# Two weight-remainder splits of a gated cross-attention block, moved from VectorE to GpSimd

## The chip, the cores and the metric

The kernel runs on one core of a Trainium2 chip, written directly against the engines: each engine has its own instruction list, executes it in order, and waits on semaphores. The metric is device time in microseconds (us) of one execution; lower is better. "DVE" is VectorE, "PE" TensorE, "ACT" ScalarE, "POOL" GpSimd, "SP" SyncE (it only issues DMAs here).

## The reference

One Flamingo-like layer: layer norm, fp8-quantised projections, self attention and cross attention with grouped heads, an fp8 output projection behind a tanh gate, and then a mixture of eight experts, two for each token. The change touches the first half only:

```python
x = x + tanh(g_xattn) * xattn(layernorm(x), ctx)   # 8 batches of 112 tokens, 375 context rows, width 512
    ln_out = ln(hidden)
    q, qx = fp8_linear(ln_out, wq), fp8_linear(ln_out, wqx)   # 16 heads of 128 each
    k, v  = fp8_linear(ln_out, wk), fp8_linear(ln_out, wv)    # 8 groups of 128 each
    kx, vx = split(ctx @ w_kv_x.T)                            # 8 groups of 128 each
    q, k, qx, kx = ln over each head's 128 channels
    cat = concat(gqa(q, k, v), gqa(qx, kx, vx))
    out = fp8(cat / smooth) @ wproj * scale
x = x + tanh(g_ffn) * experts(layernorm(x))
```

## The kernel before, in words

The attention stage walks over four group pairs (`gp` = 0 to 3) and, within each, over eight batches: 32 steps. A step projects batch `s` (`project`, six products `j` = 0 to 5: q, qx, k with v, and three chunks of the context) and attends for the batch before it, `t` = `s` - 1. Every engine has its own `step` function with a hand-written order; `passes` calls them in the same sequence on each engine.

Products are taken in fp32 by two halves. A weight block `w_raw` (in the tile `shared`) is copied by ACT into a rounded half `w_hi` (`w_high`, L600), and the remainder `w_lo` = `w_raw` - `w_hi` is a subtraction (`split_low`, L492, called from `w_low`). The weights of a group pair come in four parts, by the product that uses them (`USED`): part 0 (q) and part 1 (qx), each of 4 x 512 = 2048 elements in each of the 128 partitions; part 2, the two pieces k and v, two instructions of 4 x 256 = 1024 elements; part 3 (kx and vx, the context), one instruction of 2048. `project(s, n)` of the first step of a new group pair waits for `wh_done[n]` and `wl_done[n]`.

At a change of group pair two steps are special. The last step of the old group pair has `change == "old"`, the first step of the next has `change == "new"`. There are three such boundaries. In the kernel before DVE makes all four remainders there: part 0 in the middle of the "old" step, part 1 ahead of `sums(s, 5)`, part 2 behind `scale(s, 5)`, and part 3 in the "new" step, behind `sums(s, 1)`. Only in the very first step of the stage does POOL make part 2.

What DVE does around these places: `sums` (L859) adds up the squares of a projected head, `scale` (L868) multiplies by the reciprocal deviation, `rounded` (L918, L920, L923, L925, L928) rounds the attention output of batch `t` to fp8, `max_self` (L874) and `max_cross` (L888) take maxima of scores, `norm_self` (L880, L882) and `norm_cross` (L893, L895) scale the softmax.

What POOL does in each step: `c_low(s, k)` for k = 0, 1, 2 (L566, the remainder of a context chunk of 500 elements in each partition), each followed by `rstd(s, j)`, which is an addition `va` (L556, it waits for `sums(s, j)`) and a power `rs` (L560); then `rstd` 3, 4 and 5. `scale(s, j)` on DVE waits for `rs`, and PE's transposes of the heads (`turn`) wait for `scale`: `turn(t, 3)`, between `project(s, 1)` and `project(s, 2)`, waits for `scale(t, 5)`.

PE's order in a step: `project(s,0)`, `turn(t,0)`, `turn(t,1)`, `project(s,1)`, `turn(t,2)`, `turn(t,3)`, `project(s,2)`, `score_self(t)`, `score_cross(t,0)`, `score_cross(t,1)`, `turn(t,4)`, `project(s,3)`, `turn_self(t)` and so on (L718 are the matmuls of products 0 to 2, L727 those of 3 to 5, L747 and L751 `turn`, L759 and L766 the scores).

SP fetches the weights of the next group pair (`load_w`) behind the waits for all `wh_done` and `wl_done` of the current one, and behind the context loads and the output stores of the first two batches.

Of the kernel before, what the change touches and what calls it, by code (L numbers as in the profile page):

```python
# [369 lines left out]
def flat(ap):  # L370
    return ap.rearrange("p a b -> p (a b)")
# [17 lines left out]
def attention(nc, c, sb, ps, sem, ctxT, wproj, catd, vec, ident, mhalf, epst, xq, smi,  # L389
# [73 lines left out]
    def passes(eng, step):  # L463

        step(0, 0, None, 0, "first", None)

        def batches(gp):
            s0 = gp * B  # L470
            with eng.Fori(0, 2) as i:
                s = s0 + 2 * i
                step(s + 1, 1, s, gp + 1, None, None)
                step(s + 2, 0, s + 1, gp + 1, None, i)
            step(s0 + 5, 1, s0 + 4, gp + 1, None, 2)
            step(s0 + 6, 0, s0 + 5, gp + 1, None, 3)
            step(s0 + 7, 1, s0 + 6, gp + 1, "old", None)

        with eng.Fori(0, GP - 1) as gp:
            batches(gp)  # L480
            step(gp * B + B, 0, gp * B + 7, gp + 1, "new", None)
        s0 = (GP - 1) * B
        with eng.Fori(0, 3) as i:
            s = s0 + 2 * i
            step(s + 1, 1, s, None, None, None)
            step(s + 2, 0, s + 1, None, None, None)
        step(s0 + 7, 1, s0 + 6, None, None, None)
        step(None, 0, s0 + 7, None, None, None)

    def split_low(eng, n):  # L490
        for lo, hi in USED[n]:
            last = eng.tensor_tensor(w_lo[:, :, lo:hi], w_raw[:, :, lo:hi], w_hi[:, :, lo:hi].bitcast(F32),  # L492
                                     ALU.subtract)
        return last

    @block.sync
    def _(sp):
        def load_w(gp):
            for n in range(len(USED)):
                sp.wait_ge(wl_done[n], gp)  # L500
                sp.wait_ge(wh_done[n], gp)
            for k in range(KB):
                weights.fetch(sp, gp, k)

        def load_c(s, b, k):

            sp.wait_ge(ch_done, 3 * s + k + 1)
            sp.wait_ge(cl_done, 3 * s + k + 1)
            sp.dma_start(c_raw[:, k, :, :], ctxT[b, k]).then_inc(c_in_done[k], 16)

        def store(st):
            sp.wait_ge(ct_done, st + 1)
            sp.dma_start(catd[st], cat[:, :]).then_inc(cat_out, 16)

        sp.sem_inc(cat_out, 16)


        for gp in range(GP):
            s0 = gp * B
            for b in range(2):  # L520
                for k in range(NC):
                    load_c(s0 + b, b, k)
                if gp > 0:
                    store(s0 + b - 2)
            if gp + 1 < GP:
                load_w(gp + 1)
            else:


                for n in range(len(USED)):  # L530
                    sp.wait_ge(wl_done[n], GP)
                    sp.wait_ge(wh_done[n], GP)
                for n in range(4):
                    sp.dma_start(shared[:, n * D:(n + 1) * D], wproj[0, n]).then_inc(wp_load[n], 16)
                sp.wait_ge(cat_out, 16 * (B + 1))
                sp.dma_start(cat_tile(shared), catd[0:B].rearrange("b p n -> p b n")
                             ).then_inc(cat_load[0], 16)
            with sp.Fori(2, B) as b:
                for k in range(NC):
                    load_c(s0 + b, b, k)  # L540
                store(s0 + b - 2)
        store(GP * B - 2)
        store(GP * B - 1)
        sp.wait_ge(cat_out, 16 * (GP * B + 1))

    @block.gpsimd
    def _(pool):
        pool.sem_inc(cl_done, 3)
        pool.sem_inc(va_done, 6)
        pool.sem_inc(rs_done, 6)  # L550

        def rstd(s, j):

            rows, lo, hi = STAT[j]
            pool.wait_ge(rd_done, 6 * (s + 1) + j + 1)
            pool.tensor_tensor(va[0:rows, lo:hi], ss[0:rows, lo:hi], epst[0:rows, lo:hi],  # L556
                               ALU.add).then_inc(va_done, 1)
            pool.wait_ge(va_done, 6 * (s + 1) + j + 1)
            pool.wait_ge(ln_done, 6 * s + j + 1)
            pool.tensor_tensor(rs[0:rows, lo:hi], va[0:rows, lo:hi], mhalf[0:rows, lo:hi],  # L560
                               ALU.pow).then_inc(rs_done, 1)

        def c_low(s, k):
            pool.wait_ge(ch_done, 3 * (s + 1) + k + 1)
            pool.wait_ge(pj_rdy, 6 * s + 4 + k)
            pool.tensor_tensor(flat(c_lo[:, k, :, :]), flat(c_raw[:, k, :, :]),  # L566
                               flat(c_hi[:, k, :, :]).bitcast(F32), ALU.subtract).then_inc(cl_done, 1)

        def w_low(g, n):

            pool.wait_ge(wh_done[n], g + 1)
            split_low(pool, n).then_inc(wl_done[n], 1)

        def step(s, par, t, g, change, k):
            if change == "first":
                w_low(g, 2)
            if s is None:
                return
            for j in range(3):
                c_low(s, j)  # L580
                rstd(s, j)
            for j in range(3, 6):
                rstd(s, j)

        passes(pool, step)

    @block.scalar
# [240 lines left out]
    def _(v):  # L828
# [10 lines left out]
        def smooth_of(g):  # L839
            v.wait_ge(ya_done, 2 * B * g + 2)  # L840
            v.tensor_copy(smg[:, :], smi[:, bass.ds(g, 1), :].rearrange("p a b -> p (a b)"))

        def w_low(g, n):

            v.wait_ge(wh_done[n], g + 1)
            split_low(v, n).then_inc(wl_done[n], 1)
# [8 lines left out]
        def sums(s, j):  # L855
            rows, lo, hi = STAT[j]
            v.wait_ge(pj_done, 6 * (s + 1) + j + 1)
            v.wait_ge(va_done, 6 * s + j + 1)
            v.tensor_reduce(ss[0:rows, lo:hi],  # L859
                            sq[0:rows, j % 2, 0:(hi - lo) * HD].rearrange("p (h d) -> p h d", d=HD),  # L860
                            AX, ALU.add).then_inc(rd_done, 1)
# [9 lines left out]
        def max_self(t):  # L871
            v.wait_ge(ss_rdy, t + 2)
            v.wait_ge(es_done, t + 1)
            v.tensor_reduce(nmax[0:T, 0:HP], p_self[0:T, 0:HP * T].rearrange("p (h d) -> p h d", d=T),  # L874
                            AX, ALU.max, negate=True).then_inc(ms_done, 1)
# [54 lines left out]
        def step(s, b_next, t, g, change, k):  # L930

            A, Q = s is not None and change != "first", t is not None
            if A: sums(s, 0)
            if A: sums(s, 1)
            if change == "new": w_low(g, 3)
            if Q: max_self(t)
            if A: scale(s, 0)
            if Q: max_cross(t, 0)
            if Q: max_cross(t, 1)
            if Q: norm_self(t)  # L940
            if Q: norm_cross(t, 0)
            if Q: norm_cross(t, 1)
            if Q: take_self(t)
            if A: sums(s, 2)
            if Q: take_cross(t, 0)
            if Q: max_cross(t, 2)
            if A: scale(s, 1)
            if Q: take_cross(t, 1)
            if Q: max_cross(t, 3)
            if A: scale(s, 2)  # L950
            if A and b_next is not None: inputs(s + 1, b_next)
            if Q: norm_cross(t, 2)
            if Q: norm_cross(t, 3)
            if k is not None: weights.means(v, g, k)
            if change == "old": w_low(g, 0)
            if A: sums(s, 3)
            if Q: smoothed(t, 0)
            if Q: take_cross(t, 2)
            if Q: take_cross(t, 3)
            if A: scale(s, 3)  # L960
            if A: sums(s, 4)
            if Q: smoothed(t, 1)
            if A: scale(s, 4)
            if change == "old": w_low(g, 1)
            if A: sums(s, 5)
            if A: scale(s, 5)
            if change == "old": w_low(g, 2)
            if Q: rounded(t)
            if change == "new": smooth_of(g)
            if change == "first":  # L970
                w_low(g, 0)
                w_low(g, 1)
                w_low(g, 3)
                smooth_of(g)
                for j in range(6):
                    sums(s, j)
                    if j > 0:
                        scale(s, j - 1)
                    if j == 3:
                        inputs(s + 1, b_next)  # L980
                scale(s, 5)
# [736 lines left out]
```

## Time and profile before

| | |
|---|---|
| median of 3 runs | 1292.58 us (1290.19 to 1293.03) |
| the profiled execution | 1290.19 us, its span 1288.5 us |
| mean granted TensorE clock over the span | 0.95 |
| attention stage, about 57 to 872 us of the span | PE busy 770.71 of 814.70 us, DVE 643.90, ACT 520.72, POOL 353.05 |

A profile row gives the start or the sum in us, the duration, the engine, the line of the kernel and the tiles written and read. What stands in brackets behind a row of the timeline is how long the engine sat idle before it and what ended that wait. A row's duration runs from the start of the instruction to its end; when an engine is held up after it has begun an instruction, the hold-up is inside that duration.

### The profile page before, as it was taken

The page shows a single profiled execution, that of the slowest core. Times are in us where ns is not written, and L with a number is a line of the kernel's source. Part 1 is how long each engine was busy: PE and PEld are TensorE (multiplying, and loading weights), DVE is VectorE, ACT ScalarE, POOL GpSimd, SP SyncE. Part 2 cuts the span into 40 slices and gives each one's busy share as a digit, 9 for nine tenths or more (in the row PEclk, how much of TensorE's full clock was granted, in tenths as well). Part 3 has the DMA queues.
Part 4 walks back from the last instruction along what each step waited for, and adds up shares of the span by engine and source line. Part 5 has one row for each costly group of instructions (what it writes and reads, how often), then busy time and mean ns, then how long its engine had stood idle before and what let it go on. Part 6 is the DMA issues. An engine that isn't in the chain of part 4 may idle for free. (4 is left out here: it accounts for less than half of the span.)

```text
span 1288.5 us, 22449 instructions
## 1 busy us (share of the span) xinstructions
PE 1128.0 (88%) x5792; PEld 912.7 (71%) x5792; DVE 862.1 (67%) x1742; ACT 698.1 (54%) x1747; POOL 478.4 (37%) x608
## 2 busy tenths in 40 slices
PE   1089999989999989999998999996999449999996
PEld 1078777767787767877776788884887337777885
DVE  7968778886888787878888887775444555646100
ACT  7955677844757765567674664652122303333342
POOL 3074344343443443434434444440000202656432
PEclk9589999999999999999999999998999659999999
DMA  4041111114111113211111411102464606766220
GB/s 189 24 164 47 31 42 45 40 33 164 52 42 31 47 33 146 67 31 55 40 32 32 137 47 31 54 16 71 151 201 148 212 25 188 212 176 179 56 41 1
DMA packets 51715, 107.36 MB, mean 83 GB/s; under 512 B 5984, under 2 KB 26464, under 8 KB 49568
## 3 DMA queue, kind: packets, MB, share of 16 engines
q1 hardware_dynamic: 46912, 97.00, 23.3%
q0 software_dynamic: 4704, 9.18, 3.1%
q8 instruction: 45, 0.74, 0.2%
q14 instruction: 54, 0.44, 0.1%
HBM read 91.48 MB, written 16.52 MB: 84 GB/s over the span
## 5 line engine op out<-in xcount | busy, mean ns | idle before, releaser
L718 PE MATMUL p_proj<-w_hi,xqs 128*112 128x256 f32 (+1 forms) x512 | 173.8, 358 | 56.9 <-DVE w_lo L492 47.6
L566 POOL TENSOR_TENSOR c_lo<-c_raw,c_hi 128x500 fp32r<-128x500 f32 x96 | 122.2, 1273 | 174.9 <-ACT c_hi L606 174.9
L727 PE MATMUL p_proj<-w_hi,c_hi 128*125 128x512 f32 x384 | 167.5, 436 | 9.2 <-DVE w_lo L492 8.2
L556 POOL TENSOR_TENSOR va<-ss,epst 112x4 f32<-112x4 f32 (+2 forms) x192 | 75.7, 394 | 262.3 <-DVE ss L859 262.2
L718 PE MATMUL p_proj<-w_lo,xqs 128*112 128x256 f32 (+1 forms) x512 | 164.0, 339 | 0.0
L560 POOL TENSOR_TENSOR rs<-va,mhalf 112x4 f32<-112x4 f32 (+2 forms) x192 | 153.5, 800 | 18.0 <-POOL va L556 5.8
L727 PE MATMUL p_proj<-w_lo,c_hi 128*125 128x512 f32 x384 | 153.5, 400 | 0.0
L727 PE MATMUL p_proj<-w_hi,c_lo 128*125 128x512 f32 x384 | 153.4, 399 | 0.0
L718 PEld LDWEIGHTS p_proj<-w_hi,xqs 128*112 128x112 f32 x512 | 90.2, 176 | 73.5 <-issue 55.5
L859 DVE TENSOR_REDUCE ss<-sq 112x4 f32<-112x512 f32 (+2 forms) x192 | 96.0, 503 | 54.6 <-ACT sq L627 53.7
L655 ACT ACTIVATE pcross<-p_cross,nmax 112x375 f32<-112x375 f32 x128 | 73.1, 573 | 80.9 <-DVE nmax L888 79.8
L718 PEld LDWEIGHTS p_proj<-w_lo,xqs 128*112 128x112 f32 x512 | 90.5, 177 | 11.7
L766 PE MATMUL p_cross<-kxT,qxT 128*112 128x375 f32 x256 | 98.0, 485 | 0.0
L1127 PE MATMUL p_acc<-p_hi,p_catr 128*128 128x512 f32 x224 | 88.5, 395 | 9.1 <-DVE p_lo L1166 9.1
L727 PEld LDWEIGHTS p_proj<-w_hi,c_hi 128*125 128x125 f32 x384 | 72.8, 189 | 28.9 <-issue 10.3
L627 ACT ACTIVATE sq<-p_proj 112x512 f32<-112x512 f32 (+2 forms) x192 | 90.3, 471 | 0.0
L1127 PE MATMUL p_acc<-p_lo,p_catr 128*128 128x512 f32 x224 | 88.1, 393 | 0.0
L156 ACT ACTIVATE shared<-shared,w_mean,wsc 128x128 f32<-128x128 f32 (+1 forms) x160 | 65.9, 486 | 39.6 <-DVE w_mean L140 39.6
L727 PEld LDWEIGHTS p_proj<-w_lo,c_hi 128*125 128x125 f32 x384 | 72.9, 190 | 18.0
L727 PEld LDWEIGHTS p_proj<-w_hi,c_lo 128*125 128x125 f32 x384 | 72.4, 188 | 18.2
L792 PE MATMUL p_out<-pcrossT,valx 125*128 125x224 f32 x384 | 83.1, 352 | 0.0
L911 DVE TENSOR_TENSOR yb<-p_out,smg 128x448 bf16<-128x448 f32 x64 | 39.7, 620 | 56.6 <-PE p_out L792 56.6
(232 smaller groups left out, 2711.3 us busy)
## 6 DMA issues: line engine op xcount, KB each, us to landing
c_raw<-in_ctxT SPq DMA_DIRECT2D x96, 250.0 KB, 2.6
shared<-in_w_in SPq DMA_DIRECT2D x16, 1024.0 KB, 9.1
shared<-in_wproj SPq DMA_DIRECT2D x32, 256.0 KB, 3.0
raw_g<-in_Wg SPq DMA_DIRECT2D x8, 1024.0 KB
raw_u<-in_Wu SPq DMA_DIRECT2D x8, 1024.0 KB, 7.6
raw_d<-in_Wd SPq DMA_DIRECT2D x8, 1024.0 KB, 5.7
cat_scratch<-cat SPq DMA_DIRECT2D x32, 224.0 KB, 2.0
shared<-cat_scratch SPq DMA_DIRECT2D x2, 1792.0 KB, 8.5
```

The lines of the kernel that those rows point to most:

```text
L156: act.activation(cols, cols, ACT.Identity, bias=mean, scale=self.wsc[:, n, block_k])
L556: pool.tensor_tensor(va[0:rows, lo:hi], ss[0:rows, lo:hi], epst[0:rows, lo:hi], ALU.add).then_inc(va_done, 1)
L560: pool.tensor_tensor(rs[0:rows, lo:hi], va[0:rows, lo:hi], mhalf[0:rows, lo:hi], ALU.pow).then_inc(rs_done, 1)
L566: pool.tensor_tensor(flat(c_lo[:, k, :, :]), flat(c_raw[:, k, :, :]), flat(c_hi[:, k, :, :]).bitcast(F32), ALU.subtract).then_inc(cl_done, 1)
L627: act.activation(sq[0:rows, j % 2, 0:n], bank[0:rows, 0:n], ACT.Square, scale=float(HD) ** -0.5).then_inc(pj_done, 1)
L655: act.activation(pcross[0:T, h, :], p_cross[0:T, h % 2, 0:TC], ACT.Exp, bias=nmax[0:T, 4 + h:5 + h], accum_out=lsum[0:T, 4 + h:5 + h]).the ...
L718: m = pe.matmul(bank[0:T, o:o + w], xqs[:, n, k, :], (w_hi, w_lo)[i % 2][:, k, lo:lo + w], start=(i == 0), stop=(i == 2 * KB - 1))
L727: m = pe.matmul(bank[0:CT, :], a[:, ch, k, :], w[:, k, CKX:CV], start=(i == 0), stop=(i == 3 * KB - 1))
L766: pe.matmul(p_cross[0:T, h % 2, 0:TC], qxT[:, h * T:(h + 1) * T], kxT[:, h // HPG, :], start=True, stop=True).then_inc(sx_rdy, 1)
L792: m = pe.matmul(p_out[:, HPG * T:2 * HPG * T], valx[0:CT, par, k, g * P:(g + 1) * P], flat(pcrossT[0:CT, k, HPG * g:HPG * (g + 1), :]), st ...
L859: v.tensor_reduce(ss[0:rows, lo:hi], sq[0:rows, j % 2, 0:(hi - lo) * HD].rearrange("p (h d) -> p h d", d=HD), AX, ALU.add).then_inc(rd_don ...
L1127: m = pe.matmul(acc[:, j, :], catr[:, n % 2, j * P:(j + 1) * P], w[:, n % 2, :], start=(first and part == 0), stop=(last and part == 1), s ...
```

## The change

POOL makes part 3 in the "new" step, behind `c_low(s, 1)` and `rstd(s, 1)`, and part 2 at the end of the "old" step, behind `rstd(s, 5)`. DVE's two calls go. Parts 0 and 1 stay on DVE where they were. The arithmetic, the semaphores and what waits on them stay.

```diff
@@ pool step
             for j in range(3):
                 c_low(s, j)
                 rstd(s, j)
+                if j == 1 and change == "new":
+                    w_low(g, 3)
             for j in range(3, 6):
                 rstd(s, j)
+            if change == "old":
+                w_low(g, 2)
@@ vector step
             if A: sums(s, 0)
             if A: sums(s, 1)
-            if change == "new": w_low(g, 3)
             if Q: max_self(t)
             if A: scale(s, 0)
...
             if change == "old": w_low(g, 1)
             if A: sums(s, 5)
             if A: scale(s, 5)
-            if change == "old": w_low(g, 2)
             if Q: rounded(t)
             if change == "new": smooth_of(g)
```

## Rows read from the trace of the kernel before

**Rows 1.** Busy time of each engine over the span (first part of the page).
```profile
PE 1128.0 (88%) x5792; PEld 912.7 (71%) x5792; DVE 862.1 (67%) x1742; ACT 698.1 (54%) x1747; POOL 478.4 (37%) x608
```

**Rows 2.** Waits of PE, 57 to 900 us: total us, times, longest.
```profile
PE p_proj L718 <- DVE w_lo L492: 47.6, 7, 40.9
PE p_proj L727 <- DVE w_lo L492: 8.2, 3, 2.7
...
PE p_out L789 <- DVE pcrossT L906: 6.8, 13, 0.9
```

**Rows 3.** Timeline of PE at the first boundary: start, duration, instruction, idle before.
```profile
266.43 0.34 PE L718 MATMUL p_proj<-w_hi,xqs 128*112 128x256 f32 x1 [1.52 <-DVE w_lo L492]
...
273.67 0.76 PE L727 MATMUL p_proj<-w_hi,c_hi 128*125 128x512 f32 x1 [2.74 <-DVE w_lo L492]
274.22 0.63 PE L727 MATMUL p_proj<-w_lo,c_hi 128*125 128x512 f32 x1
...
276.73 0.39 PE L727 MATMUL p_proj<-w_lo,c_hi 128*125 128x512 f32 x1
```

**Rows 4.** Busy time and granted clock in two stretches: PE, PEld, DVE, ACT, POOL, clock.
```profile
274.00:276.00 2.00, 2.00 (x6) 1.50 (x6) 1.51 (x1) 1.45 (x8) 2.00 (x3) 0.50 0.00 0
...
280.00:282.00 2.00, 2.00 (x10) 1.49 (x10) 2.00 (x4) 0.66 (x2) 1.89 (x3) 1.00 0.00 0
```

**Rows 5.** Timeline of DVE at the first boundary.
```profile
263.59 0.43 DVE L868 TENSOR_TENSOR nkx<-nkx,rs 125x256 f32<-125x256 f32 x1 [1.08 <-POOL rs L560]
263.93 2.35 DVE L492 TENSOR_TENSOR w_lo<-shared,w_hi 128x1024 fp32r<-128x1024 f32 x2
266.20 1.46 DVE L918 TENSOR_SCALAR yb<-yb 128x896 bf16<-128x896 bf16 x1
267.69 0.40 DVE L920 TENSOR_SCALAR ye<-yb 128x896 uint16<-128x896 uint16 x1
...
271.03 2.28 DVE L492 TENSOR_TENSOR w_lo<-shared,w_hi 128x2048 fp32r<-128x2048 f32 x1
...
274.49 1.74 DVE L868 TENSOR_TENSOR nq<-nq,rs 112x512 f32<-112x512 f32 x1 [0.64 <-POOL rs L560]
...
277.26 0.62 DVE L882 TENSOR_TENSOR pself<-pself,linv 112x448 f32<-112x448 f32 x1
```

**Rows 6.** Timeline of POOL at the first boundary.
```profile
262.86 0.70 POOL L560 TENSOR_TENSOR rs<-va,mhalf 125x2 f32<-125x2 f32 x1
265.95 1.45 POOL L566 TENSOR_TENSOR c_lo<-c_raw,c_hi 128x500 fp32r<-128x500 f32 x1 [2.40 <-ACT c_hi L606]
270.61 2.77 POOL L556 TENSOR_TENSOR va<-ss,epst 112x4 f32<-112x4 f32 x1 [3.20 <-DVE ss L859]
...
274.43 1.26 POOL L566 TENSOR_TENSOR c_lo<-c_raw,c_hi 128x500 fp32r<-128x500 f32 x1
275.64 0.65 POOL L556 TENSOR_TENSOR va<-ss,epst 112x4 f32<-112x4 f32 x1
276.37 1.01 POOL L560 TENSOR_TENSOR rs<-va,mhalf 112x4 f32<-112x4 f32 x1
```

**Rows 7.** Timeline of DVE in the stage's first step.
```profile
62.83 4.49 DVE L492 TENSOR_TENSOR w_lo<-shared,w_hi 128x2048 fp32r<-128x2048 f32 x2 [0.27 <-ACT w_hi L600]
68.32 3.41 DVE L492 TENSOR_TENSOR w_lo<-shared,w_hi 128x2048 fp32r<-128x2048 f32 x1 [1.00 <-ACT w_hi L600]
71.66 2.30 DVE L841 COPY smg<-smi 128x8 f32<-128x8 f32 x1
```

**Rows 8.** Timeline of POOL in the stage's first step.
```profile
66.57 7.36 POOL L492 TENSOR_TENSOR w_lo<-shared,w_hi 128x1024 fp32r<-128x1024 f32 x2 [46.51 <-ACT w_hi L600]
```

**Rows 9.** Groups of POOL by line: busy us, mean ns.
```profile
L566 POOL TENSOR_TENSOR c_lo<-c_raw,c_hi 128x500 fp32r<-128x500 f32 x96 | 122.2, 1273 | 174.9 <-ACT c_hi L606 174.9
...
L556 POOL TENSOR_TENSOR va<-ss,epst 125x2 f32<-125x2 f32 x96 | 20.4, 212 | 247.7 <-DVE ss L859 247.7
```

**Rows 10.** Timeline of SP, the fetch of the next weights.
```profile
297.16 2.06 SPq L129 DMA_DIRECT2D shared<-in_w_in  x4
```

## The prediction, on record before the changed kernel ran

> **What bounds the kernel now.** I read the engines' busy time first, then PE's waits in the attention stage, then the timelines of PE, DVE and POOL around one change of group pair, and last the only place where POOL already makes a weight remainder. PE is busy 88% of the span, DVE 67% and POOL 37% [rows 1]. So PE sets the pace, and the 4.6 us that leave DVE at each boundary are worth only what PE waits for them; POOL has idle time enough, but the question is when it is idle.
>
> PE's waits name the remainder [rows 2]. The 40.9 us are the start of the stage, where the change does nothing. The three waits of L727, 8.2 us together, are `project(s, 3)` at the three boundaries, waiting for part 3. At the first boundary [rows 3] PE waits 1.52 us for part 2 and 2.74 us for part 3. Behind the last wait the granted clock is 0.50, that is the lower of the two levels, 1.2 GHz, and it is back at 1.00 later [rows 4]; a matmul of that stretch takes 0.63 us until, at 276.73, one takes 0.39 again [rows 3]. In the timeline six of them stand 0.43 us apart where 0.23 is usual (up to nine at the other boundaries), so the clock adds 1.2 to 1.8 us. What could be won at each boundary is thus 1.52 + 2.74 + about 1.2 = 5.5 us, and 16 us over the three. The other two boundaries repeat the first (three waits of L727, 8.2 us in sum, 2.7 the longest [rows 2]), so I work out one and take it three times.
>
> **The change, part by part.** The removal from DVE: two instructions of 1024 elements, 2.35 us, and one of 2048, 2.28 us, a boundary [rows 5].
>
> The price on POOL. No row shows a POOL subtraction of 2048 elements. Two rows bound it. The 500-element one takes 1.27 us and a two-element addition 0.21 us [rows 9], so an element costs (1.27 - 0.21) / 498 = 2.1 ns and 2048 cost 4.6 us. The two of 1024 elements in the first step took 7.36 us together [rows 8], but with DVE's subtractions in between: DVE's first pair ended at 67.32 and its third ran until 71.73 us [rows 7]. Read as turns taken, POOL's first ran from 67.32 to 69.59 (2.27 us), DVE's from there to 71.73 (2.14 of its usual 2.28), and POOL's second from 71.73 to 73.93 (2.2 us); the tiny copy on DVE at 71.66, 2.30 us long, ended with it. So 1024 elements cost 2.2 to 2.3 and 2048 about 4.5 us. That is twice DVE's price. The upper bound is 7.4 us for 2048, if the recorded duration is all work; the lower 4.1 us, from the slope between 1.27 us at 500 and 2.2 us at 1024. I take 4.5, which both readings give.
>
> Turns taken. The same is seen at the boundary. POOL's `c_lo` at 265.95 stretches DVE's L918, which ends 0.26 us behind it and takes 1.46 us [rows 5, 6] where 0.39 is its usual time; DVE's `w_lo` at 271.03 holds POOL's four-element `va` from 270.61 to 273.38; `c_lo` at 274.43 holds DVE's L868 of 274.49 until 275.69 and beyond that it needs 0.54 us; then `va` waits for it. Whoever is held goes next.
>
> The Trainium skill ("SBUF — State Buffer", section on the two separate sides) says the same: the port pair of VectorE and GpSimd is an exclusive lock for a whole instruction, also against a VectorE instruction with two SBUF inputs. It speaks against this change, and its "GPSIMD Engine Reference" (elementwise comparison) gives 4497 ns for 2048 fp32 elements on GpSimd and 2293 ns on VectorE; by that the sum below would stay within 0.1 us a boundary. The trace agrees with the second figure (2.28 us) and shows no row for the first.
>
> Now the new order at the first boundary. Both waits of the moved calls on `wh_done` are long fulfilled, so only POOL's own order and the turns count.
> - Part 2 can't start before `rs` of `rstd(s, 5)` ends, at 263.56 [rows 6]. First piece, 2.27: to 265.83. It starts a moment before DVE's `scale(s, 5)` (263.59), as `c_lo` does at 274.43, and holds it; that takes 0.4: to 266.2. Second piece, 2.2: to 268.4. So `project(s, 2)` starts at about 268.6 where it was 266.43: 2.1 us later. `turn(t, 3)`, which waits for `scale(s, 5)`, goes from 264.4 to 266.4 and stays hidden.
> - DVE's L918 gets the turn: to 268.7. Queued behind part 2 on POOL is `c_low(s, 0)`, 1.25: to 269.95. L920 is held and ends at 270.2. From the end of L920 to the start of `va` took 270.61 - 268.09 = 2.52 us (rest of `rounded`, `sums(s, 0)`): 272.75.
> - `va` now finds no `w_lo` on DVE and takes 0.2: to 272.95. This is all that the relief of DVE brings POOL: 0.43 us against 273.38. From there to the end of `rs` of `rstd(s, 1)` it took 277.38 - 273.38 = 4.0: 276.95.
> - Part 3 can start there. DVE's L882, 1.03 us behind the end of L868, comes at nearly the same moment and takes 0 to 0.6 us of it: 277.4. Part 3, 4.5: to 281.9. PE follows 0.36 us behind the remainder, as now (271.03 + 2.28 to 273.67): 282.3.
>
> So `project(s, 3)` starts 8.6 us later than at 273.67. Of this, 2.2 us is the slower engine, and 6.4 us the later start, 277.4 instead of 271.03, because part 3 stands behind `rstd(s, 1)` and the whole chain before it behind part 2. PE has nothing to do between `turn(t, 4)` and then. The lower clock stays about as it is: the wait is longer, the number of matmuls until it rises again I take as the same, with 0 to 0.5 us more. Given back: after the wait DVE and ACT are ahead, and PE's small waits in the rest of the step go, 0 to 0.5 us. Behind part 3 on POOL stand `c_low(s, 2)`, needed by `project(s, 5)` 8 us later, and `rstd(s, 2)`, whose `sums` waits for PE anyway: nothing. On DVE the `norm_cross` instructions are held during part 3, but PE's `turn_self` follows `project(s, 3)`, 3.5 to 4 us long, in which they catch up: nothing; without that cover they would cost 1 us. SP's fetch stands at 297.16 [rows 10], far behind part 3's semaphore: it moves with the rest, and no DMA is added.
>
> Sum: 3 x 8.6 - 3 x 0.1 = 25.5 us, or 1290.19 + 25.5 = 1315.7 for the profiled execution. That one was the fastest of three, 2.4 us under the median of 1292.58, so the median of the changed kernel lies between 1315.7 and 1318.1; I take 1317.
>
> **The rivals.**
> - No turns: the two engines run side by side, and the hold-ups above are something else. Then part 2 ends at 263.56 + 4.5 = 268.1, `c_low(s, 0)` at 269.4, and with 1.3 for `rstd(s, 0)`, 1.3, 1.3 for `rstd(s, 1)` and 4.5, part 3 ends at 277.7: 4.4 us later than now, 13 in all, 1304. Against it stand four stretched rows at one boundary [rows 5, 6], each ending within 0.3 us of the other engine's instruction or 0.54 behind it.
> - POOL's large subtraction costs its recorded 3.7 us for 1024 elements. Then part 2 adds 2.9 and part 3 2.9 us more: 14.4 us a boundary, 43 in all, 1333. Against it: the copy of eight elements that took 2.30 us on DVE beside it [rows 7], which only makes sense if it was held.
> - Absorbed, no change: PE makes up the delay from later waits. The largest of its waits in the stage that isn't for a weight remainder is 6.8 us in 13 times, the longest 0.9 [rows 2], and 8.6 would be needed behind each boundary.
> - The other side, faster: the remainders are done on POOL before PE asks, and all of the 5.5 us at a boundary go, 1290.19 - 16.4 = 1274. It decides at part 3's end: sooner than 273.31 is a gain. With both POOL prices at nothing, `rounded` would begin at 264.0, `sums(s, 0)` end at about 267.9 and `rstd(s, 1)` at about 272.0, so the prices together could be at most 1.3 us; DVE itself needs 4.6. Only if POOL's rows say nothing of these instructions can it be.
>
> The Trainium skill's "Perfetto Trace Analysis" (on ScalarE and DVE operations) reminds that moving work between GpSimd and VectorE might not help as they share a read port; as a rule it would leave the time about the same, which is the absorbed case.
>
> **How the numbers follow.** Forecast 0.82; no turns 0.07; the dearer subtraction 0.05; absorbed 0.04; faster 0.02. The forecast's own spread: price of part 3 4.1 to 5.2 (-0.4 to +0.7), part 2 the same again, L882's turn -0.5, clock and catching up -0.5 to +0.5: 7.2 to 10.5 us a boundary, 1312 to 1322 with the 2.4 us between runs. No more than 2 in 10 are to be left out; the errors of such a hand-made schedule run both ways, so I go to 1305 (the case without turns just touches it) and 1328. About 0.2% (2.6 us) is what a measurement of this kernel can tell from no change. Slower 0.94, the same 0.04, faster 0.02.
>
> **What would show each step.** PE's wait for `w_lo` should be put down to POOL: about 1.7 us before L718 (or more, if `turn(t, 3)` runs earlier) and 8 to 9.5 us before L727, three times. POOL should show L492 six times with 1024 elements, 2.2 to 2.3 us, and three times with 2048, 4.5 us (5.0 with L882's turn inside); DVE's L868 of `scale(s, 5)` should take 2.6 us there instead of 0.43, and L895 some 4 to 5 us during part 3. `va` of `rstd(s, 0)` should fall from 2.77 to 0.2 us. The expert stage should have the same length. I would be wrong if part 3 ended before about 278 us on the old time axis, that is if POOL reached it sooner than `rstd(s, 1)` lets me think, or if the two engines' instructions overlapped.

## The result, and the profile after

The changed kernel takes 1314.07 us in the median (1311.06 to 1315.18, 4 runs), the kernel before 1292.01 us beside it (1290.19 to 1293.03). The ratio is 1.0162, with a 95% interval of 1.0147 to 1.0175: slower by 22 us. Over all 13 runs of the changed kernel on record the median is 1312.82 us. The profiled execution took 1314.62 us, its span 1312.9 us, 24.4 us more than before.

Busy time of each engine over the span, and busy time and clock (0.50, the lower level) at the start of `project(s, 3)`:

```profile
PE 1133.0 (86%) x5792; PEld 918.1 (70%) x5792; DVE 877.1 (67%) x1733; ACT 699.7 (53%) x1747; POOL 497.0 (38%) x617
```
```profile
280.00:282.00 2.00, 1.81 (x4) 1.48 (x5) 1.96 (x4) 0.00 (x0) 1.05 (x1) 0.50 0.00 0
```

DVE has 9 instructions less than in [rows 1] and is busy 15 us more. What left it took 13.9 us; the rows count hold-up as busy time, so a busier DVE here is a DVE that is held.

PE's waits in the attention stage of the changed kernel, 57 to 920 us (total us, times, longest):

```profile
PE p_proj L722 <- DVE w_lo L492: 43.3, 4, 41.1
PE p_proj L731 <- POOL w_lo L492: 18.8, 3, 7.0
...
PE p_tr L755 <- DVE nkx L872: 4.6, 3, 1.7
```

The lines moved by 4, so L731 is the L727 of [rows 2]. PE's three waits for part 3 were 8.2 us and are 18.8, and they are POOL's now. They understate it: PE is also slow before the wait. At the first boundary `project(s, 2)` ran at the lower clock and took 3.44 us where it took 1.96 before, which shortens the wait behind it and costs nothing more, as POOL sets its end.

PE at the first boundary:

```profile
264.97 0.54 PE L755 MATMUL p_tr<-ident,nkx 125*128 125x125 f32 x3 [1.71 <-ACT kT L643]
267.19 0.53 PE L722 MATMUL p_proj<-w_hi,xqs 128*112 128x256 f32 x1 [1.69 <-ACT sq L631]
...
272.68 0.48 PE L755 MATMUL p_tr<-ident,nkx 125*128 125x125 f32 x3
280.19 0.76 PE L731 MATMUL p_proj<-w_hi,c_hi 128*125 128x512 f32 x1 [7.03 <-POOL w_lo L492]
280.75 0.63 PE L731 MATMUL p_proj<-w_lo,c_hi 128*125 128x512 f32 x1
...
284.41 0.39 PE L731 MATMUL p_proj<-w_lo,c_hi 128*125 128x512 f32 x1
```

The second wait, 1.69 us, is credited to ACT's second square of the step. But `project(s, 2)` needs only the first, and what it waits for besides, POOL's L492 pair, ended at 267.05 (next fence), 0.14 us ahead of it: a wait for several semaphores can carry the wrong name. Compare with [rows 3]: PE waits three times here, and the last wait is 7.03 us.

POOL at the first boundary:

```profile
261.53 0.70 POOL L560 TENSOR_TENSOR rs<-va,mhalf 125x2 f32<-125x2 f32 x1
262.19 4.86 POOL L492 TENSOR_TENSOR w_lo<-shared,w_hi 128x1024 fp32r<-128x1024 f32 x2
267.01 1.40 POOL L566 TENSOR_TENSOR c_lo<-c_raw,c_hi 128x500 fp32r<-128x500 f32 x1
271.18 0.20 POOL L556 TENSOR_TENSOR va<-ss,epst 112x4 f32<-112x4 f32 x1 [2.77 <-DVE ss L863]
...
275.34 4.50 POOL L492 TENSOR_TENSOR w_lo<-shared,w_hi 128x2048 fp32r<-128x2048 f32 x1
279.80 1.25 POOL L566 TENSOR_TENSOR c_lo<-c_raw,c_hi 128x500 fp32r<-128x500 f32 x1
```

DVE at the first boundary:

```profile
262.25 2.58 DVE L872 TENSOR_TENSOR nkx<-nkx,rs 125x256 f32<-125x256 f32 x1 [1.08 <-POOL rs L560]
264.76 2.54 DVE L922 TENSOR_SCALAR yb<-yb 128x896 bf16<-128x896 bf16 x1
267.33 1.33 DVE L924 TENSOR_SCALAR ye<-yb 128x896 uint16<-128x896 uint16 x1
...
275.26 6.27 DVE L886 TENSOR_TENSOR pself<-pself,linv 112x448 f32<-112x448 f32 x1
...
281.63 0.42 DVE L899 TENSOR_SCALAR pcross<-pcross,linv 112x375 f32<-112x375 f32 x1
```

The axis has slid by 1.33 us against [rows 6], so times are best counted from the end of `rs` of `rstd(s, 5)`: 263.56 before, 262.23 now. `project(s, 3)` started 10.11 us behind it and starts 17.96 us behind it, 7.85 us later; at the second boundary it is 7.84. Three times 7.85 is 23.6 of the 24.4 us. The rest is small terms: this execution was 1.33 us ahead when it came to the first boundary, and lost 2.0 us between the third `project(s, 3)` and the end of the stage.

### The profile page after: what moved, and what is told of

It reads as the page before. It is cut to its first block and busy times, and to the rows that moved or that the text cites. A ratio compares the mean times of both kernels' runs of the same rounds, so it can differ in the third digit from the quotient of the medians.

```text
span 1312.9 us, 22452 instructions
## 1 busy us (share of the span) xinstructions
PE 1133.0 (86%) x5792; PEld 918.1 (70%) x5792; DVE 877.1 (67%) x1733; ACT 699.7 (53%) x1747; POOL 497.0 (38%) x617
## 5 line engine op out<-in xcount | busy, mean ns | idle before, releaser
L722 PE MATMUL p_proj<-w_hi,xqs 128*112 128x256 f32 (+1 forms) x512 | 177.6, 364 | 57.4 <-DVE w_lo L492 43.3
L731 PE MATMUL p_proj<-w_hi,c_hi 128*125 128x512 f32 x384 | 167.6, 437 | 19.9 <-POOL w_lo L492 18.8
L556 POOL TENSOR_TENSOR va<-ss,epst 112x4 f32<-112x4 f32 (+2 forms) x192 | 65.4, 341 | 281.6 <-DVE ss L863 281.6
L722 PE MATMUL p_proj<-w_lo,xqs 128*112 128x256 f32 (+1 forms) x512 | 167.5, 345 | 0.0
L731 PE MATMUL p_proj<-w_hi,c_lo 128*125 128x512 f32 x384 | 153.5, 400 | 0.0
L731 PE MATMUL p_proj<-w_lo,c_hi 128*125 128x512 f32 x384 | 153.2, 399 | 0.0
L722 PEld LDWEIGHTS p_proj<-w_hi,xqs 128*112 128x112 f32 x512 | 93.0, 182 | 74.1 <-issue 55.9
L722 PEld LDWEIGHTS p_proj<-w_lo,xqs 128*112 128x112 f32 x512 | 93.2, 182 | 11.8
L731 PEld LDWEIGHTS p_proj<-w_hi,c_hi 128*125 128x125 f32 x384 | 72.7, 189 | 39.3 <-issue 21.0
L731 PEld LDWEIGHTS p_proj<-w_lo,c_hi 128*125 128x125 f32 x384 | 72.8, 189 | 18.0
L731 PEld LDWEIGHTS p_proj<-w_hi,c_lo 128*125 128x125 f32 x384 | 72.4, 189 | 18.3
```

The costliest lines, as they stand in the source:

```text
L722: m = pe.matmul(bank[0:T, o:o + w], xqs[:, n, k, :], (w_hi, w_lo)[i % 2][:, k, lo:lo + w], start=(i == 0), stop=(i == 2 * KB - 1))
L731: m = pe.matmul(bank[0:CT, :], a[:, ch, k, :], w[:, k, CKX:CV], start=(i == 0), stop=(i == 3 * KB - 1))
```

## The experiments

All were compared with the kernel before on the same chip. "Behind" means behind the end of `rs` of `rstd(s, 5)` at the first boundary.

**Part 2 alone on POOL.**

```diff
-                if j == 1 and change == "new":
-                    w_low(g, 3)
@@ vector step
             if A: sums(s, 1)
+            if change == "new": w_low(g, 3)
```

> Only part 2 goes to POOL; part 3 stays on DVE behind sums(s, 1). My theory (turns taken, and a chain through DVE's rounded): part 2 ends about 2.1 us later, the held rounded instructions bring sums(s, 1) to an end about 0.6 us later at most, DVE's 2.35 us are gained back only in part, and project(s, 3) starts 1.9 us later than before at each boundary: 5.8 us in all, about 1298. Rival, only the price of the engine counts (2.2 us for part 2, nothing for DVE's held instructions): DVE would reach part 3 2.3 us earlier and project(s, 3) would start 1 to 2 us earlier than before, 1287 to 1290.

Measured: 1298.11 us, ratio 1.0048 (1.0028 to 1.0067). PE in its trace:

```profile
267.72 0.53 PE L720 MATMUL p_proj<-w_hi,xqs 128*112 128x256 f32 x1 [1.69 <-ACT sq L629]
...
274.77 0.47 PE L729 MATMUL p_proj<-w_hi,c_hi 128*125 128x512 f32 x1 [1.10 <-DVE w_lo L492]
```

`project(s, 3)` starts 12.02 us behind, 1.9 later than before. DVE was relieved of 2.35 us and is nevertheless late for part 3: its rounding was held.

**Part 3 alone on POOL.**

```diff
-            if change == "old":
-                w_low(g, 2)
@@ vector step
             if A: scale(s, 5)
+            if change == "old": w_low(g, 2)
```

> Only part 3 goes to POOL, to the place it has in the change; part 2 stays on DVE. My theory: va of rstd(s, 0) starts at 270.61 as before but is no longer held, and from there the 9.0 us of the changed kernel lead to project(s, 3): at 279.6 instead of 273.67, 5.9 us a boundary, 17.8 in all, about 1310. Rival, the two moved parts cost alike because each is simply twice as dear on POOL (2.2 us each): about 6.6 us in all, 1299.

Measured: 1309.72 us, ratio 1.0137 (1.0118 to 1.0156).

```profile
279.51 0.76 PE L729 MATMUL p_proj<-w_hi,c_hi 128*125 128x512 f32 x1 [8.68 <-POOL w_lo L492]
```

16.04 us behind, 5.9 later than before. In the traces the two halves of the change add up: 1.9 + 5.9 = 7.8. (Between the medians they give 7.0 and 18.6 us, 3.6 more than the whole change.) Part 3 is three quarters of the loss, though both are the same number of elements.

**The later place without the slower engine.** Part 3 stays on DVE, behind `scale(s, 0)`.

```diff
             if A: sums(s, 1)
-            if change == "new": w_low(g, 3)
             if Q: max_self(t)
             if A: scale(s, 0)
+            if change == "new": w_low(g, 3)
```

> Nothing on POOL: part 3 stays on DVE but stands behind scale(s, 0), which waits for rs of rstd(s, 0). It is the later place without the slower engine. My theory: scale(s, 0) ends at about 273.7, part 3 at 276.0, project(s, 3) starts at 276.4, 2.7 us later than before, 8 us in all, about 1300. If the place were nothing and the engine all, it would stay at 1292.

Measured: 1301.09 us, ratio 1.0071 (1.0052 to 1.0089).

```profile
274.90 0.76 PE L727 MATMUL p_proj<-w_hi,c_hi 128*125 128x512 f32 x1 [5.26 <-DVE w_lo L492]
```

12.63 us behind, 2.5 later, and it costs more than that: `turn_self` starts 3.5 us later at this boundary, since all twelve matmuls of `project(s, 3)` ran at the lower clock. The median is 10.0 us above the kernel before, against 18.6 for part 3 on POOL: about half of what part 3 loses comes with a later place in the list alone. (The place in the change is later still, behind `rstd(s, 1)`.)

**The change, with `rounded` of the old step's batch moved.**

```diff
-            if Q: rounded(t)
+            if Q and change != "old": rounded(t)
...
             if Q: norm_cross(t, 3)
+            if change == "new": rounded(t - 1)
```

(`rounded` counts on a semaphore of its own for it.)

> The change as it is, but the rounding of the old group pair's last-but-one batch (rounded, 2.6 us alone, 5.8 us held) moves from the end of DVE's old step behind norm_cross(t, 3) of the new step. My theory: in the changed kernel POOL idles 2.77 us ahead of va of rstd(s, 0) because sums(s, 0) stands behind rounded; that idle goes, part 3 starts and ends about 3 us earlier, and 7 to 10 us of the 22 come back: 1304 to 1307. Rival, POOL's own work is the whole chain (price of its instructions): no change against 1314.

Measured: 1310.87 us, ratio 1.0131 (1.0102 to 1.0161), a miss: 3 us back instead of 7 to 10, and its interval overlaps that of the change.

```profile
279.89 0.76 PE L732 MATMUL p_proj<-w_hi,c_hi 128*125 128x512 f32 x1 [5.64 <-POOL w_lo L493]
...
301.06 0.46 PE L723 MATMUL p_proj<-w_hi,xqs 128*112 128x512 f32 x1 [3.44 <-issue]
```

The expected part did happen: POOL's idle ahead of `va` is gone and `project(s, 3)` starts 15.1 us behind (its `rs` ended at 264.80), 2.9 earlier than in the change. But at the head of the next loop pass PE idles 3.44 us where it was 1.08, and then runs at the lower clock. Busy time, clock and DMA share and GB/s of the 2 us before:

```profile
296.00:298.00 2.00, 1.62 (x8) 1.26 (x8) 0.72 (x3) 0.26 (x1) 0.89 (x2) 1.00 0.98 332
```

SP's list has the store of that batch ahead of three context loads. The store now waits until 294 us, and the loads fall on the loop's end.

**The same, with the stores behind both batches' loads.**

```diff
                     load_c(s0 + b, b, k)
-                if gp > 0:
-                    store(s0 + b - 2)
+            if gp > 0:
+                store(s0 - 2)
+                store(s0 - 1)
```

> The change with rounded moved (the kernel of 1310.87) and, in SP's list, the output stores of the last two batches placed behind the context loads of both first batches. In the former the store waits for the moved rounding until 294 us and the loads of batch 1 (1 MB in all) land at 294 to 298, when PE fetches the code of its next loop pass: its idle there is 3.44 us instead of 1.08, with the lower clock behind it. If that collision ate the gain, its two occurrences of 2.4 us and 1.3 us of clock come back: 1303 to 1305. Rival, the late rounding itself delays PE: no change, 1311.

Measured: 1305.03 us, ratio 1.0095 (1.0078 to 1.0112), as expected in size, with a less clean cause than that:

```profile
297.54 0.46 PE L724 MATMUL p_proj<-w_hi,xqs 128*112 128x512 f32 x1 [2.83 <-issue]
```

The idle at the head is 2.83, not 1.08; only 0.6 to 0.85 us of it at each of the two heads was the loads. The fall of the clock behind it is gone at the second head only: at the first the granted clock is 0.50 again from 299 to 301 us. And PE's waits for part 3 are 12.9 us in place of 14.8.

**Part 3 on DVE ahead of `rounded`, nothing on POOL.**

```diff
             if change == "old": w_low(g, 2)
+            if change == "old": w_low(g, 3)
             if Q: rounded(t)
...
-            if change == "new": w_low(g, 3)
```

> The kernel before with one call moved on DVE: part 3 directly behind part 2, ahead of rounded. PE's wait for part 3 (2.74 us and the lower clock behind it) goes. My theory: DVE's list is the second bound of the boundary, since PE's turn_self at 277.94 starts 0.06 us behind DVE's L882; that instruction stays where it is, so PE waits there instead and the time stays within 1 us a boundary of before, 1289 to 1293. Rival, PE's wait for the remainder is all that counts: 3.9 us a boundary, 11.8 in all, 1280.

Measured: 1291.66 us, ratio 0.9995 (0.9985 to 1.0005).

```profile
276.16 0.59 PE L773 MATMUL p_tr<-ident,pself 112*112 112x112 f32 x4 [3.83 <-DVE pself L882]
```

PE's wait for part 3 is gone from the list and comes back as 3.83 us ahead of `turn_self`, which starts 13.99 us behind, 0.4 earlier than before. DVE's list was the second bound: in the kernel before, L882 ended at 277.88 [rows 5], and `turn_self` began at 277.94.

**Part 3 at the head of POOL's new step**, part 2 on DVE.

```diff
@@ pool step
+            if change == "new":
+                w_low(g, 3)
             for j in range(3):
                 c_low(s, j)
```

> Part 2 stays on DVE; part 3 goes to POOL but to the head of its new step, ahead of c_low(s, 0), where POOL idles. If the later place were all of the loss, project(s, 3) would start at about 271 us and the kernel gain 3 us a boundary, 1283. My theory of turns taken: POOL gets its turn between DVE's two part 2 pieces at 265.1 and holds the second until 269.6, rounded, sums and the maxima come late, and PE waits for turn_self until about 281: 3 us a boundary later than before, 1301, still less than the 1310 of part 3 alone behind rstd(s, 1).

Measured: 1295.27 us, ratio 1.0022 (1.0013 to 1.0032). The rival's 1283 is out, and so is my 1301. POOL, DVE and PE, in this order:

```profile
264.09 5.03 POOL L492 TENSOR_TENSOR w_lo<-shared,w_hi 128x2048 fp32r<-128x2048 f32 x1 [0.94 <-ACT w_hi L602]
```
```profile
263.53 6.68 DVE L492 TENSOR_TENSOR w_lo<-shared,w_hi 128x1024 fp32r<-128x1024 f32 x2
```
```profile
270.35 0.53 PE L720 MATMUL p_proj<-w_hi,xqs 128*112 128x256 f32 x1 [5.84 <-DVE w_lo L492]
```

The turns came as thought (DVE's pair takes 6.68 us instead of 2.35), but `turn_self` was only 2.0 us late. That is what DVE's list gives: 4.33 us of hold-up on its pair, less the 2.28 us of part 3 that it no longer makes; I had left the second out. The other place of part 3 on POOL had ratio 1.0137: the place matters more than the choice of POOL.

**The turns alone.** Everything stays on DVE, and POOL makes part 2 once more behind `rstd(s, 5)`, into a tile that nobody reads.

```diff
+            if change == "old":
+                pool.wait_ge(wh_done[2], g + 1)
+                for n, (lo, hi) in enumerate(USED[2]):
+                    pool.wait_ge(sp_self, 2 * g - 2 + n)
+                    pool.tensor_tensor(spare[:, :, :], w_raw[:, :, lo:hi], w_hi[:, :, lo:hi].bitcast(F32),
+                                       ALU.subtract).then_inc(sp_self, 1)
```

> The kernel before, with all four parts on DVE, and POOL making part 2 once more, into a tile that nobody reads, at the place it has in the change (behind rstd(s, 5)). Only the turns between the two engines can cost anything. My theory: POOL's two pieces hold scale(s, 5) and then DVE's own part 2, which ends 4 to 5 us later, and PE's project(s, 2) and all behind it with it: 12 to 15 us in all, 1304 to 1307. Rival, the engines run side by side: nothing, 1292, or 1 us where c_low(s, 0) starts later.

Measured: 1303.30 us, ratio 1.0090 (1.0074 to 1.0107), just under what I expected. POOL, DVE and PE:

```profile
263.74 4.94 POOL L593 TENSOR_TENSOR spare<-shared,w_hi 128x1024 fp32r<-128x1024 f32 x2
```
```profile
263.81 2.64 DVE L879 TENSOR_TENSOR nkx<-nkx,rs 125x256 f32<-125x256 f32 x1 [1.09 <-POOL rs L565]
266.38 5.56 DVE L494 TENSOR_TENSOR w_lo<-shared,w_hi 128x1024 fp32r<-128x1024 f32 x2
```
```profile
272.09 0.52 PE L729 MATMUL p_proj<-w_hi,xqs 128*112 128x256 f32 x1 [4.97 <-DVE w_lo L494]
```

Work on an idle engine, for nobody, costs 11.4 us. That settles the rival without turns.

**A new order on DVE, nothing on POOL.** Part 1 goes ahead of `smoothed(t, 1)`, part 2 ahead of `scale(s, 5)`, part 3 to the head of the new step, `rounded` and SP's stores as above.

```diff
+            if change == "new": w_low(g, 3)
             if A: sums(s, 0)
...
+            if change == "old": w_low(g, 1)
             if Q: smoothed(t, 1)
             if A: scale(s, 4)
-            if change == "old": w_low(g, 1)
             if A: sums(s, 5)
-            if A: scale(s, 5)
             if change == "old": w_low(g, 2)
+            if A: scale(s, 5)
```

> The kernel before, nothing on POOL, DVE's list reordered at the boundary: part 1 ahead of smoothed(t, 1) where DVE idles 1.28 us, part 2 between sums(s, 5) and scale(s, 5) where it idles 1.08, part 3 at the head of the new step, rounded of the old step's batch behind norm_cross(t, 3), and the stores placed as in the run before. My theory: all three waits of PE (0.72, 1.52, 2.74) and the lower clock go, 4.4 + 1.2 us a boundary, less about 1 us for turn_self and the late rounding: 4.6 us, 14 in all, 1276 to 1281. Rival, DVE is bound through the boundary whatever its order, and PE waits elsewhere: 1290.

Measured: 1281.75 us, ratio 0.9916 (0.9899 to 0.9932); faster than both, just outside what I expected.

```profile
263.49 0.54 PE L753 MATMUL p_tr<-ident,nkx 125*128 125x125 f32 x3 [1.30 <-DVE nkx L870]
...
283.24 0.64 PE L791 MATMUL p_out<-pselfT,val 112*128 112x224 f32 x2 [0.86 <-DVE pcrossT L908]
...
287.38 0.46 PE L720 MATMUL p_proj<-w_hi,xqs 128*112 128x512 f32 x1 [2.37 <-issue]
```

No wait for a remainder is left at the boundaries. The loss is again at the loop's end.

**The same order, `rounded` and the stores in place.** Only the calls of the parts and of `scale(s, 5)` are moved, as in the diff above:

```diff
+            if change == "new": w_low(g, 3)
             if A: sums(s, 0)
...
+            if change == "old": w_low(g, 1)
             if Q: smoothed(t, 1)
...
             if change == "old": w_low(g, 2)
+            if A: scale(s, 5)
             if Q: rounded(t)
```

> The same new order of parts 1, 2 and 3 on DVE, but rounded at its old place at the end of the old step and SP as before. My theory: PE's waits for the parts go and come back as a wait for DVE's L882 ahead of turn_self, less the 1.3 to 2 us of idle that the new order fills on DVE: 1 to 2 us a boundary gained, 1286 to 1289. Rival, the order alone is worth all of the gain: 1282.

Measured: 1285.15 us, ratio 0.9952 (0.9935 to 0.9968), a little better than expected. PE still waits 1.16 us for part 3 at the first boundary, and then 2.00 us for L882 ahead of `turn_self` (3.83 with part 3 moved alone).

**The new order, `rounded` in two.** The stores stay behind both batches' loads. The clamp goes into a tile `yc` behind `norm_cross(t, 3)`, the other four instructions ahead of `smoothed(t, 1)`.

```diff
-            if change == "new": rounded(t - 1)
+            if change == "new": clamped(t - 1)
...
+            if change == "new": rounded_rest(t - 1)
             if Q: smoothed(t, 1)
```

> The reordered kernel of 1281.75, in which rounded of the old step's batch stands behind norm_cross(t, 3) and PE waits 0.9 us for take_cross(t, 3) and then 2.4 us at the head of the loop, where it waited 1.2. Here only the clamp (0.4 us, into a tile of its own) stays there, and the other four instructions stand ahead of smoothed(t, 1), where DVE idles. My theory: PE's wait before the loop's end is what lays its head's idle bare, so both go at the two loop heads and the first at the third boundary: 2 us a boundary and the lower clock at the heads, 5 to 8 in all, 1274 to 1277. Rival, the idle at the head comes from the stores that land just before it: 1 us a boundary, 1279.

Measured: 1274.76 us, ratio 0.9865 (0.9849 to 0.9882), 17 us faster than the kernel before, as expected.

```profile
266.32 0.54 PE L754 MATMUL p_tr<-ident,nkx 125*128 125x125 f32 x3 [1.30 <-DVE nkx L872]
274.26 0.59 PE L776 MATMUL p_tr<-ident,pself 112*112 112x112 f32 x4 [0.17 <-DVE pself L886]
287.99 0.46 PE L721 MATMUL p_proj<-w_hi,xqs 128*112 128x512 f32 x1 [1.24 <-issue]
```

These are all of PE's idle times over 0.1 us from 262 to 289 us that the timeline marks; the head is back at 1.24.

## Why the prediction was right, step by step

- **The price on POOL.** 4.5 us for 2048 elements, taken from rows of 500 and 1024: measured 4.50. The "GPSIMD Engine Reference" of the Trainium skill (elementwise comparison) gives 4497 ns; the trace agrees. The recorded mean of 3.7 us for 1024 was hold-up, as read: without DVE in the way the first of the two pieces of 1024 takes 2.37 of the pair's 4.86 us.
- **Part 2's end and `project(s, 2)`.** Predicted 4.8 and 5.0 us behind, measured 4.82 and 4.96. The held L868 (now L872) was to take 2.6 us and takes 2.58; the two rounding instructions are held 2.1 and 0.9 us beyond their usual time. The Trainium skill ("SBUF — State Buffer", the two separate sides) calls the shared port pair an exclusive lock for a whole instruction; these rows agree, and the redundant part 2 shows what it costs, 11.4 us.
- **The relief of DVE.** `va` of `rstd(s, 0)` falls from 2.77 to 0.20 us, as said, and brings POOL no more than that.
- **Part 3's start.** Predicted 13.8 us behind (277.4), measured 13.1. Here is the mis-sized term: I gave 0.5 us to a turn of DVE's L882 ahead of part 3. POOL got its turn instead, and L882 was held for 6.27 us. The sign named for it, 4 to 5 us for L895, failed with it: L895 (L899 now) took 0.42, and the instruction ahead of it bore the hold-up. The rest, 0.2 us, lies ahead of L920's end, predicted 6.64 us behind and measured 6.43, since `c_low(s, 0)` came sooner; from there to `va` it took 2.52 us, as predicted.
- **The shift of `project(s, 3)`.** 8.6 us predicted, 7.85 measured, for that reason. Part 3 alone gave 5.9 and part 2 alone 1.9. Of part 3's 5.9, 2.5 are the place (shown with DVE doing the work there), the rest the engine and its place behind `rstd(s, 1)`, not measured apart.
- **A sign that failed.** PE's wait before L727 was to be 8 to 9.5 us and is 7.03, 5.76 and 6.04. At the first boundary 0.75 us of the difference is the earlier part 3, and 1.5 us the lower clock in `project(s, 2)`, which the prediction didn't have. It made no difference to the time, as POOL's end sets the start of `project(s, 3)`.
- **The clock.** I took the lower clock's cost as unchanged, with 0 to 0.5 us more. The twelve matmuls of `project(s, 3)` take 4.68, 4.34 and 5.25 us at the three boundaries, where they took 4.27, 4.42 and 4.41: 0.4 more on average. At the first boundary PE was at 1.2 GHz behind the wait and at 2.4 GHz (0.39 us a matmul) again at 284.41.
- **The cover of what was costed at nothing.** L895 stood behind the held L886 until 281.6 and still had its work done before `project(s, 3)` ended; SP's fetch moved with the rest. That this cover is thin was seen where it was used up: in the kernels with `rounded` moved whole, PE waited 0.55 to 1.0 us for `take_cross`.
- **The sum.** 25.5 us predicted, 24.4 in the span, 22.1 between the medians; 1317 against 1314.07. The expert stage kept its length: its first matmul moved by the same 24.4 us (897.32 to 921.72). One sum was off: the lower ends of the forecast's own spread add up to 6.8 us a boundary, not 7.2; the measured 7.85 lies inside either. Of the rivals, no turns, absorbed, the dearer subtraction and faster are each excluded by a row above.

What the prediction left unsaid, since it asked only for the change, is that the 5.5 us a boundary it called winnable could not be had by taking away PE's waits alone: behind them stood DVE's L882, which ended 0.06 us before PE needed it (0.2 at the other two boundaries), and removing the wait for part 3 won nothing (ratio 0.9995). With DVE's whole list reordered and the rounding in two, 17 us over the three boundaries were there to be had, without POOL.

## What to carry to other kernels

Before work is moved to the idle one of two engines that take turns at a port, count what it will hold there, not only what it takes: 4.9 us of it in the wrong stretch cost 3.8 us a boundary even when nobody waited for its result. A wait of the bounding engine is worth only the distance to the next bound, and that is read from how closely the next releaser stands behind it. Work that is not urgent (here a rounding ahead of a store) belongs into the idle times of its engine, in pieces if need be; moving it whole cured one wait and made two others.

## What the runs showed of the hardware

- The engine that is held mostly goes next, but not always. DVE's L886 (112x448), which began 0.08 us before POOL's 4.50 us subtraction, was held by it and then also by the `c_lo` behind it: it ended at 281.5, 0.5 us behind `c_lo`'s end at 281.05. With part 3 alone on POOL it was the same, 6.27 us again, and 6.04 us with the rounding moved. In all nine places where part 3 on POOL held this instruction, it lost its turn to the `c_lo`, while L872 and L922 got theirs between two POOL instructions. Why that one doesn't is open.
- PE's idle at the head of the outer loop is 0.8 to 1.5 us when PE has had no wait in the last product before the loop's end, and 2.4 to 2.8 us when it has waited there for `take_cross` (0.55 to 1.0 us), and 3.4 to 3.7 with such a wait and 332 GB/s (first head) or 270 GB/s (second) of loads just before. In all the kernels here the long idle stood with such a wait, and it went with it in the last one; but each time the whole rounding was late too, so this is a coincidence seen in three kernels, and the mechanism is not shown. The Trainium skill ("Runtime: NRT & Kernel Launch", instruction fetch mechanics) says that a taken branch whose target isn't already in the instruction memory forces a fetch by DMA before execution goes on; that would fit an idle at this place, but not why a wait before it makes it longer, and no run here shows it.
- With the same order of work the lower clock does not come at the same instruction at each boundary. At the first boundary of the changed kernel `project(s, 2)` and part of `project(s, 3)` ran at it, at the other two the scores between them as well, and at the third all of `project(s, 3)`; still the start of `project(s, 3)` is the same to 0.01 us, because POOL sets it.
